# Experts loaded and split in place during the attention, a table of 12800 rows, gathered rows in the experts' memory

## The reference, cut to what matters

```python
h = take(W.T, x)                                # 16 x 256 token ids below 12564, rows of W.T: (50257, 256) f32
h = h + attn(layernorm(h))                      # six layers
h = h + ffn(layernorm(h))                       # eight experts, top two, and one shared expert

# one attention layer, b = 16 sequences of 256 tokens, d = 256
n = layernorm(x) * gamma[l] + beta[l]
q, k, v = split(n @ w_qkv[l])
q, k = softmax(q, axis=1), softmax(k, axis=2)
out = einsum('bic,bij->bjc', q, einsum('bic,bjc->bij', k, v))
x = out @ w_out[l] + b_out[l] + x

# an expert: w1, w2 (256, 512), w3 (512, 256)
y = silu(x @ w1) * (x @ w2) @ w3
```

## Time and profile before

| what | value |
|---|---|
| median of 3 runs | 1548.67 us (1547.54 to 1548.8) |
| the profiled execution's own time | 1553.85 us |
| its span, first to last instruction | 1552.1 us |
| granted TensorE clock, mean | 0.931 |
| busy share of the span | PE 83%, DVE 66%, POOL 63%, ACT 53% |
| DMA traffic | 160.28 MB, mean 103 GB/s |
| first product of the attention | 195.50 us |
| last round of the attention's loop before its tail | about 957 us |

### The profile page before, as it was taken

How to read it: one execution, slowest core, us unless ns; L and a number is a source line. 1 busy time by engine, 2 the same in 40 slices (tenths; PEclk the granted TensorE clock), 3 DMA queues, 4 the chain that set the end, 5 groups by cost and what they waited for, 6 DMA issues and landing times. The chain is left out here.

```text
span 1552.1 us, 37797 instructions
## 1 busy us (share of the span) xinstructions
PE 1293.1 (83%) x11400; PEld 1098.9 (71%) x11401; DVE 1027.6 (66%) x2634; ACT 829.2 (53%) x2251; POOL 971.6 (63%) x967
## 2 busy tenths in 40 slices
PE   3520079999999999999999997777788999999996
PEld 2410058888888888888888886666666888888885
DVE  3245668888888888888888886754445444444443
ACT  2132157778777877877787775734432223232221
POOL 0037589888888988988898888355442233333333
PEclk8855589999999999999999999898998999999998
DMA  9988423352244235325323334653334244443441
GB/s 325 398 307 299 122 57 63 68 132 61 61 91 108 59 63 132 62 60 125 74 61 76 80 68 79 105 96 94 93 93 128 49 65 59 60 66 55 63 61 14
DMA packets 356716, 160.28 MB, mean 103 GB/s; under 512 B 283953, under 2 KB 340273, under 8 KB 356657
## 3 DMA queue, kind: packets, MB, share of 16 engines
q1 hardware_dynamic: 321810, 119.56, 32.5%
q0 software_dynamic: 20064, 25.32, 9.0%
q10 hardware_dynamic: 14784, 14.68, 2.7%
HBM read 46.08 MB, written 44.21 MB: 58 GB/s over the span
## 5 line engine op out<-in xcount | busy, mean ns | idle before, releaser
L708 PE MATMUL bank<-hT,Wc 128*128 128x256 f16 x2304 | 286.2, 275 | 112.0 <-DMA hT<-hhl 106.4
L708 PEld LDWEIGHTS bank<-hT,Wc 128*128 128x128 f16 x2304 | 226.8, 99 | 140.3 <-issue 112.7
L670 POOL DMA_INDIRECT out_rows<-h0b,payin x78 | 121.1, 1553 | 240.3 <-DVE h0b L1363 217.1
L1032 ACT ACTIVATE silu<-bank 128x512 f32<-128x512 f32 x110 | 65.6, 596 | 229.1 <-PE bank L805 218.0
L805 PE MATMUL bank<-xTg,W12h 128*128 128x256 f16 x1248 | 187.2, 273 | 0.0
L579 POOL TENSOR_TENSOR h0b<-h0b,rows 128x512 f32<-128x512 f32 x96 | 121.9, 1270 | 94.0 <-issue 47.3
L1305 DVE SCALAR_TENSOR_TENSOR gT<-bank,silu 128x512 f32<-128x512 f32 x110 | 76.0, 691 | 155.8 <-ACT silu L1032 148.6
L708 PE MATMUL bank<-Wc,MT 128*128 128x256 f16 x1152 | 144.0, 276 | 19.6 <-DVE MT L1171 19.6
L821 PE MATMUL bank<-W3h,gThl 128*128 (+1 forms) x880 | 132.2, 283 | 25.9 <-DVE gThl L1311 22.5
L708 PE MATMUL bank<-khl,eqT 128*128 128x256 f16 x1152 | 141.5, 272 | 5.6 <-issue 0.2
L708 PE MATMUL bank<-Wc,hT 128*128 128x256 f16 x1152 | 141.8, 273 | 0.0
(11 more groups left out here) (153 smaller groups left out, 2938.8 us busy)
## 6 DMA issues: line engine op xcount, KB each, us to landing
VW<-in_L_tok_W SPq DMA_DIRECT2D x28, 512.0 KB, 6.5
FST<-in_L_ffn_ew SPq DMA_DIRECT2D x24, 512.0 KB
emb_rows<-h0b ACTq DMA_DIRECT2D x14, 512.0 KB, 8.1
emb_rows<-VR ACTq DMA_DIRECT2D x14, 512.0 KB, 9.5
Wc<-Wn SPq DMA_DIRECT2D x48, 128.0 KB, 2.2
Wst<-in_L_attn_w_qkv SPq DMA_DIRECT2D x6, 768.0 KB, 4.9
h_rows<-X SPq DMA_DIRECT2D x4, 1024.0 KB, 4.8
X<-h_rows POOLq DMA_DIRECT2D x8, 512.0 KB, 8.2
```

What stands on the lines that cost most here:

```text
L670: pool.indirect_dma_start(out=out_rows, out_offset=bass.IndirectOffsetOnAxis(ap=got(j % PAYS, w, 0, i32), axis=0), in_=yout[j % 2][:, w, : ...
L708: last = mm(to, lhs(a, k, o), moving, start=(i == 0 and k == 0), stop=(i == 2 and k == 1))
```

## The change

- Every expert's high and low parts lie in one tensor `Wall`, six chunks of 512 columns (`XCH`) per expert, high beside low. The f32 weights are loaded into the very place of their two f16 parts and split in place, chunk by chunk: 54 chunks.
- The splitting moves into the attention: one chunk an item, in the second half of layers 0 to 4 (40 items) and in the first 14 items of the last layer. ACT makes two operations of 512 columns between khl and nqmax (`expert_high`), DVE one `tensor_tensor` at the end of its round (`expert_low`).
- The loads move too: experts 0 to 2 are issued after the second transpose of the attention, one more at the end of each of the layers 0 to 3, the last two at the end of layer 4.
- The embedding uses `Wall`'s memory: five load buffers and five row buffers, a step of five chunks, a stretch of five steps (12800 rows). The gathered rows land in `G`, in the experts' memory, and the norm goes from `G` to `X`; it no longer waits for the store of `h0_rows`.
- The first layer's weights are loaded right after the last chunk. Their low parts are made by DVE instead of POOL, ahead of the first statistics.
- `padt` is half as large; the embedding's `ident`, `idrow` lie in `Wall`; the experts' stage addresses its weights with one register instead of two.

```diff
-    VBUF = 4
+    VBUF = 5
-    STRETCH = 7
+    XCH = HID
+    XPER = EXP // XCH
+    XALL = NE * XPER
+    STRETCH = 5
...
+        Wf = Wall[:, :].bitcast(f32)
+        G = Wf[:, NE * EXP - NT * D:].rearrange("p (t d) -> p t d", t=NT)
...
 # item_loop, for ACT, DVE and POOL
-                with eng.Fori(NB // 4, NB // 2) as h:
-                    pair(h, False)
+                with eng.Fori(0, quarter) as b:
+                    pair(eng.snap(b + quarter), EXPERT, b)
...
 # SP
+            for e in range(3):
+                load_expert(e)
+            more = {l: range(3 + l, 4 + l if l < DEPTH - 2 else NE) for l in range(DEPTH - 1)}
...
+                for e in more.get(l, ()):
+                    load_expert(e)
...
 # ACT, between khl and nqmax
+            def expert_high(t, kind, n):
+                act.wait_ge(s_xload, 48 * (NE if kind == LAST else layer(t) + 3))
+                act.wait_ge(s_xlo, n + 1)
+                act.wait_ge(s_wnlo, WSL * (DEPTH if kind == LAST else layer(t) + 2))
+                A(Wsc[:, :], Wf[:, bass.ds(n * XCH, XCH)], ACT.Copy, scale=WS).then_inc(s_xt, 1)
+                act.wait_ge(s_xt, n + 1)
+                A(Wall[:, bass.ds(n * (2 * XCH), XCH)], Wsc[:, :], ACT.Copy).then_inc(s_xhi, 1)
...
 # DVE, at the end of a round
+            def expert_low(n):
+                dve.wait_ge(s_xhi, n + 1)
+                V.tensor_tensor(Wall[:, bass.ds(n * (2 * XCH) + XCH, XCH)], Wsc[:, :], Wall[:, bass.ds(n * (2 * XCH), XCH)],
+                                ALU.subtract).then_inc(s_xlo, 1)
...
 # DVE, before the first statistics
+            for c in range(WSL):
+                lo = slice(c * WSN, (c + 1) * WSN)
+                dve.wait_ge(s_wnhi, c + 1)
+                V.tensor_tensor(Wn[:, 1, lo], Wsc[:, 0:WSN], Wn[:, 0, lo], ALU.subtract).then_inc(s_wnlo, 1)
...
-                dve.wait_ge(s_h0st[g], 16)
-                    last = V.tensor_scalar(X[:, t, :], X[:, t, :], mv[:, t, 0:1], rstd[:, t:t + 1], ALU.subtract, ALU.mult)
+                    last = V.tensor_scalar(X[:, t, :], G[:, t, :], mv[:, t, 0:1], rstd[:, t:t + 1], ALU.subtract, ALU.mult)
```

More of the change, by code:

```diff
@@ L305, in tower, with item_loop, pair @@
         AHEAD = 6
-        def item_loop(eng, one, lead, prepare=False, behind={}):
-            def pair(h, prep):
+        PLAIN, CUT, EXPERT, LAST = range(4)
+        def item_loop(eng, one, lead, other=True, behind={}):
+            def pair(h, kind, c=None):
                 for p in range(2):
-                    one(eng.snap(h * 2 + p), p, prep)
+                    one(eng.snap(h * 2 + p), p, kind, None if c is None else eng.snap(c * 2 + p))
+            quarter = NB // 4
             for t in range(-lead, 2):
-                one(t, t % 2, prepare and t >= 0)
-            if not prepare:
+                one(t, t % 2, CUT if other and t >= 0 else PLAIN, None)
+            if not other:
@@ L323, in item_loop @@
                 with eng.Fori(1, DEPTH - 1) as l:
[L324 to L329, removed]
[L330 to L331 removed]
+                    with eng.Fori(0, quarter) as b:
+                        pair(eng.snap(l * (2 * quarter) + b), CUT)
@@ new lines, in item_loop @@
+                    with eng.Fori(0, quarter) as b:
+                        pair(eng.snap(l * (2 * quarter) + b + quarter), EXPERT, eng.snap(l * quarter + b))
+                with eng.Fori(0, (NB - AHEAD) // 2) as b:
+                    pair(eng.snap(b + (ITEMS - NB) // 2), LAST, eng.snap(b + (DEPTH - 1) * quarter))
+            for t in range(ITEMS - AHEAD, ITEMS):
+                c = t - (ITEMS - NB) + (DEPTH - 1) * (NB // 2)
+                if other and c < XALL:
+                    one(t, t % 2, LAST, c)
+                else:
+                    one(t, t % 2, PLAIN, None)
@@ L371, in _ @@
                 load(0, j * VCH, j)
[L372 to L384, removed]
-            sp.dma_start(gw[:, :, :], gate_w.rearrange("(k p) e -> p k e", p=P)).then_inc(s_gw, 16)
-            sp.wait_ge(s_padt, 1)
-            sp.dma_start(slot_x[E * CAP:E * CAP + W2, :].rearrange("(w p) d -> p w d", p=P), padt[:, :, :]).then_inc(s_pad, 16)
-            sp.wait_ge(s_flo, NE)
             def stage(l):
@@ L542, in _ @@
                 pool.sem_inc(s_passed, 1)
-                for t in range(NT):
-                    pool.indirect_dma_start(out=X[:, t, :], out_offset=None, in_=emb_rows,
-                                            in_offset=bass.IndirectOffsetOnAxis(ap=idx[:, t:t + 1], axis=0),
-                                            bounds_check=VROWS - 1, oob_is_err=False)\
-                        .then_inc(s_gath[t // 8], 16)
+                for g in range(4):
+                    gather(g)
                 for g in range(4):
@@ L568, in _, with cut, one @@
                 pool.tensor_tensor(rstd[:, 8 * g:8 * g + 8], v, mhalf[:, 0:8], ALU.pow).then_inc(s_rstd, 1)
-                for n in range(WSL * max(g - 1, 0) // 3, WSL * g // 3):
-                    cut(n)
-            def one(t, p, prep):
+            def cut(n):
+                lo = bass.ds((n % WSL) * WSN, WSN)
+                pool.wait_ge(s_wnhi, n + 1)
+                pool.sem_inc(s_passed, 1)
+                pool.tensor_tensor(Wn[:, 1, lo], Wsc[:, 0:WSN], Wn[:, 0, lo], ALU.subtract).then_inc(s_wnlo, 1)
+            for g in range(4):
+                first_root(g)
+            def one(t, p, kind, c):
                 u, w = t + 5, t + 6
@@ L934, in cut @@
                 wait(act, s_wnlo, n)
-                A(Wsc[:, :], Wst[:, at], ACT.Copy, scale=WS).then_inc(s_wsc, 1)
+                if not (isinstance(l, int) and l < 2):
+                    act.wait_ge(s_xlo, (l - 1) * (NB // 2) + 1)
+                A(Wsc[:, 0:WSN], Wst[:, at], ACT.Copy, scale=WS).then_inc(s_wsc, 1)
                 act.wait_ge(s_wsc, n + 1)
```

193 lines of the change are left out of this document (92 added, 101 removed).

## The result

The changed kernel takes 1590.04 us (median of 4 runs, 1587.5 to 1591.62) against 1548.67: a ratio of 1.0271, with a 95% interval of 1.0257 to 1.0285. I had forecast 1546.1 with 1568 as the upper end; it is slower by 41 us. The profiled execution took 1590.88 us with a span of 1588.7, 36.6 more than before (before's profiled execution lay 5.2 us over its own median, this one 0.8).

A forecast was written before the change was run, and what follows sets the result against it. The prediction took TensorE and the ring of DVE's norm, POOL's operations and root to bound the attention. Terms -21 - 8.6 - 7 + 32 + 2 = -2.6 us gave 1551.3 profiled, 1546.1 from the median; range 1530 to 1568.

The forecast's parts named there:

- The embedding, the gathering, the first norm: Before the attention: fewer bytes, undisturbed gathers and no cut pieces save 21, 8.6 and 7 us; first product at 158.5.
- rival 4: Embedding: loads bound by a buffer's chain, not bytes, so the first gather starts at 85; +7 us, 1552; chance 0.04.
- 0 to 2 each, I take 1 for all five: Layers' ends: 1.6 MB more loads on SP's queue before the next eqT; 1 us lost in all.
- The start ... I take 1: Start of the attention: transposes of hT and eqT queue behind three experts' loads; 0 to 12 us, taken as 1.
- Rival 3: Start and layers' ends: the transposes stand behind the expert loads; +12 us more, 1557; chance 0.08.
- The items with an expert: Attention items with a splitting chunk: DVE and POOL delay each other, 8.05 becomes 8.65 us; +32 us in all (16 to 57).
- the larger counts and not the sum: Items with an expert: ACT's added delay is another ring about as long as POOL's, so the two do not add.
- The reading in which only VectorE waits: Items with an expert: POOL is not delayed by DVE's new operation; the sum would be 14 us smaller.
- The rule of the Trainium skill: Items with an expert: two-SBUF-input VectorE and SBUF-reading GpSimd instructions exclude each other throughout; one collision, 0.16 us, cited as agreeing.
- The tail: The written-out tail: four items with an expert, two of them inside a wait for `h0_rows`; +2 us.
- The shares of the forecast: Whole kernel: chances of the outcome against the kernel before: faster 0.44, same 0.20, slower 0.36.
- Rival 2: Items with an expert: the waits add and 1.1 us an item reach TensorE; +24 us, 1572; chance 0.25.

The follow-up runs named there:

- e4_fix: Changed kernel with e1_own's scratch and e2's spread loads, plus the seventh to ninth experts loaded one layer earlier each; ratio 0.9982 to the kernel before.
- e10: Changed kernel with only the first three experts' loads moved behind the turns of items 1, 3 and 5 of the first layer; ratio 1.0256 to the kernel before.
- e1_own: Changed kernel with the experts' scaled pieces in a scratch of their own instead of the cut weights' Wsc; 1567.13 us, ratio 1.0122 to the kernel before.
- e6: e4_fix with ScalarE doing one operation per expert item instead of two, the scaling left out; ratio 0.9979 to the kernel before.
- e2: Changed kernel with each later expert's three loads at three places of SyncE's order instead of together; 1572.24 us, ratio 1.0151 to the kernel before.
- e3: Changed kernel with the edits of e1_own and e2 together; 1551.3 us, ratio 1.0017 to the kernel before.
- e8: e4_fix with the scaled piece in the PSUM bank of the item's last product, VectorE subtracting behind the maximum over k; ratio 0.9860 to the kernel before.
- e7: e4_fix with the scaled piece in EQ's PSUM bank, and ScalarE's two operations and VectorE's subtraction moved within the item; ratio 1.0015 to the kernel before.

## Why the prediction was wrong

By its own steps:

- **The embedding, the gathering, the first norm: right in the mechanism, and exact by luck.** Forecast 21 + 8.6 + 7, the first product at 158.5; it came at 158.48. But the gathering began at 81.4 instead of 78, inside the range I gave and halfway to rival 4's 85. It is not that rival's cause: the DMA share was 1.06 from 60 to 79 us, so bytes did bind, and 27.9 MB were moved until then, close to the 27.6 of the working. The 3.2 us missing there were made good by the gathering (-9.6 instead of -8.6), the norm (-7.8 instead of -7) and the way from the first statistics to the first product, which I had left as it was (12.8 us instead of 14.6). Of VectorE's eight small pieces four lay beside gathers; only the first gather took 1.25 us, all others 1.00 to 1.04.
- **"0 to 2 each, I take 1 for all five": this step failed.** The five layers' ends lost 25.4 us by the transposes behind the expert loads (111.0 against 85.7 in e4_fix), 5 each. I had worked out 7.5 us of transfers at 400 GB/s and about 8 us until the next eqT, and called the difference of 0.5 us room. The transfers took 13.7 us until the last had landed, and hT stands ahead of eqT in the queue and met the same backlog first. ScalarE waits 4.2 us on the mean for it (16.8 in four) and the end costs five; TensorE's clock is at half when it comes back.
- **"The start ... I take 1": the same error,** 6.3 us, 4.5 of them by e10. My reason, that GpSimd fills the pipeline at its own pace, does not hold: TensorE waited 6.09 us for eqT. Rival 3 was this mechanism, with 12 us and a chance of 0.08; at both places together it was about 30 us (25.4 and 4.5).
- **The joint in mid-layer stands in no step: it was put at nothing, without a reason.** I costed the operations that the change adds, and not the wait on the cut pieces that comes with a shared scratch. It cost 23.5 us (e1_own). The diff shows it: the name of the scratch is in two functions, and the wait is a line in one.
- **The items with an expert: right in mechanism, near in size.** Forecast 8.65 us with VectorE 0.8 to 1.4 long and GpSimd's next operation late by 0.55 to 0.69; measured 8.58 (8.41 in the last layer), 1.26 and 0.45. Thirty us were forecast, and the items took 25.5 by e4_fix. In the changed kernel the items 10 to 14 and 81 to 90 together lost 12.7 us instead of 15.0; there the items behind a pause cannot be told from it. That ScalarE's part is only covered, "the larger counts and not the sum", e6 confirms. The reading in which only VectorE waits is out, since GpSimd's operation is longer by 0.45 us. The rule of the Trainium skill that I had quoted (SBUF — State Buffer, "Who interferes with whom") agrees in that both sides wait; but whole operations in turn would have given VectorE 0.70 + 0.69 = 1.39 us, and it took 1.26. The row on which I had let the rule rest says less than I made of it: its 0.16 us came with an overlap of 0.30.
- **The tail: +2 forecast, -2.0 measured,** which is no finding: in e1, e2 and e3 the stretch from item 90 on takes 593.2 to 595.4 us.
- **Slips of the working that change nothing of this:** 21 + 8.6 + 7 is 36.6 and not 37. At 0.3 us an item instead of 0.6 the sum is 15 us smaller and not 14. From 1546.1, rival 3 comes to 1558 and rival 4 to 1553, a microsecond more than stated. The shares of the forecast that I gave make slower 0.39 and same 0.17, not 0.36 and 0.20.

Rival 2 named waits that add, item by item; they added at the joints instead, where my sum had 2 us in all (1 at the start, 1 for the five layers' ends), and the range to 1568, drawn to reach near rival 2, had no room for more. With the measured terms in place of mine the sum is -37.0 + 6.3 (start) + 25.4 (layers' ends) + 23.5 (mid-layer) + 25.5 (items) - 2.6 (cut items) - 2.0 (tail) = +39, against 36.6 between the two spans and 41 between the medians. The 2.4 us too many are the ordinary items of e4_fix, which are longer than those of the changed kernel (213.3 and 84.2 against 211.5 and 83.5).

## What to carry to other kernels

When a change moves work to another place in a steady loop, cost the joints, where one kind of item meets the next, apart from the items: look up every scratch and semaphore that the moved work shares with what runs until then, and where in its item the engine that releases it does so. On a queue that also carries a small transfer with a deadline, put large loads in one at a time between two of them; half a microsecond of margin is none. Where two engines are both near the bound, look for an operand in another memory and for the place in the order together: with the operand in PSUM e8 won 19 us and e7 lost 5, and they differ in where the operations stand.

## What was not expected of the hardware

- Behind a pause of 3.67 us of TensorE its granted clock was 0.50 instead of 1.00, and the next 24 products took 5.7 us instead of 3.1. The joints at which ScalarE waited 3.5 us cost 4.7 each (23.5 for five).
- VectorE's cast with one SBUF operand still met GpSimd: 0.89 us on the mean, and 1.38 instead of 1.27 beside it. With one operand in SBUF and one in PSUM nothing was lost on either side (0.681 and 1.269).
- In the kernel before, each of the seven gathers that began during VectorE's operation of 2048 columns ended 0.9 us after that operation's end (1.1 in the first), as if it had been held until then: 111.71 + 2.80 = 114.51 against 111.34 + 2.29 = 113.63 in the earlier trace rows. In the changed kernel three gathers beside VectorE's subtraction of 256 columns took 1.01 to 1.04 us. Whether the size or the kind of the operation makes the difference is not known.
